# Attention with a folded projection: the scaling by 1/sum written back into PSUM, x added there, each as one VectorE operation

## The reference

```python
xn = (x - moving_mean) * jax.lax.rsqrt(moving_var + BN_EPS) * gamma + beta
q = xn @ Wq + bq
k = xn @ Wk + bk
v = xn @ Wv + bv
scores = jnp.einsum('bhid,bhjd->bhij', q, k) * d ** (-0.5)
attn = jax.nn.softmax(scores, axis=-1)
out = jnp.einsum('bhij,bhjd->bhid', attn, v)
out = out @ Wo + bo
return xn + out
```

## Time and profile before

| | us |
|---|---|
| median of 3 runs | 5316.65 |
| lowest, highest | 5316.29, 5316.69 |
| the profiled execution | 5315.75 |
| its span | 5313.9 |
| TensorE busy | 5260.1 |
| VectorE busy | 5029.7 |
| ScalarE busy | 4772.2 |
| GpSimd busy | 3642.2 |

### The profile page before, as it was taken

One profiled execution on the slowest core, in us unless ns is written; L12 is line 12 of the kernel. 1 busy time (PEld: TensorE's weight loads), 2 busy tenths in 40 slices (PEclk: granted clock), 3 DMA queues, 4 the chain that ended last, 5 costly groups with the idle time before them and its releaser, 6 DMA issues. The chain is left out here.

```text
span 5313.9 us, 177339 instructions
## 1 busy us (share of the span) xinstructions
PE 5260.1 (99%) x51224; PEld 4017.8 (76%) x51224; DVE 5029.7 (95%) x15394; ACT 4772.2 (90%) x19460; POOL 3642.2 (69%) x2056
## 2 busy tenths in 40 slices
PE   7999999999999999999999999999999999999999
PEld 5777777777777777777777777777777777777777
DVE  7999999999999999999999999999999999999998
ACT  6999999999999999999999999999999999999998
POOL 5666666666666666666666666666666666666665
PEclk9999999999999999999999999999999999999999
DMA  6777777777777777777777777777777777777776
GB/s 132 153 153 152 153 153 153 153 153 153 153 153 152 153 153 153 153 153 154 153 153 153 153 153 153 153 153 153 153 153 153 153 153 153 153 153 153 153 152 129
DMA packets 4294236, 806.27 MB, mean 152 GB/s; under 512 B 4294208, under 2 KB 4294208, under 8 KB 4294208
## 3 DMA queue, kind: packets, MB, share of 16 engines
q1 hardware_dynamic: 4294208, 805.93, 78.1%
HBM read 537.10 MB, written 268.44 MB: 152 GB/s over the span
## 5 line engine op out<-in xcount | busy, mean ns | idle before, releaser
L252 POOL TENSOR_TENSOR x_weighted<-x_in,row_weights 128x1024 f32<-128x1024 f32 x1024 | 2425.5, 2369 | 1554.9 <-issue 1159.7
L300 ACT ACTIVATE probs<-score_ps,neg_top 128x128 f32<-128x128 f32 x8192 | 2876.6, 386 | 0.0
L385 DVE SCALAR_TENSOR_TENSOR y<-o_ps,inv_sum,x_scaled_rows 128x64 f32<-128x64 f32 x8192 | 1665.5, 276 | 218.2 <-DVE inv_sum L378 213.3
L300 ACT ACTIVATION_READ_ACCUMULATOR probs<-score_ps,neg_top 128x1 f32 x8192 | 1854.2, 226 | 0.0
L461 PE MATMUL probsT_ps<-ident,probs 128*128 128x128 f32 x8192 | 1286.8, 280 | 2.5 <-ACT probs L300 2.0
L257 POOL TENSOR_TENSOR x_scaled_rows<-x_weighted,out_bias 128x512 f32<-128x512 f32 x1024 | 1216.0, 1187 | 90.7 <-POOL x_weighted L252 20.2
L392 DVE TENSOR_REDUCE row_stat<-score_ps 128x8 f32<-128x1024 f32 x1024 | 1244.2, 1215 | 6.5 <-PE score_ps L474 6.5
L474 PE MATMUL score_ps<-xT,g 64*128 64x128 f32 x16384 | 1190.8, 285 | 1.9 <-ACT g L284 1.9
L485 PE MATMUL u_ps<-probsT,x_in 128*64 128x128 f32 x16384 | 1120.6, 279 | 0.0
L474 PEld LDWEIGHTS score_ps<-xT,g 64*128 64x128 f32 x16384 | 994.6, 187 | 128.0 <-ACT g L284 5.0
L501 PE MATMUL g_ps<-xT,w_g 128*128 128x512 f32 x2048 | 1051.0, 595 | 2.9 <-DVE xT L425 2.9
(11 more groups left out here) (65 smaller groups left out, 1332.1 us busy)
## 6 DMA issues: line engine op xcount, KB each, us to landing
x_quads<-in_x SPq DMA_DIRECT2D x4096, 64.0 KB, 2.2
x_in<-in_x SPq DMA_DIRECT2D x1024, 256.0 KB, 2.9
out<-y SPq DMA_DIRECT2D x1024, 256.0 KB, 2.7
norm_row<-in_L_conv_gamma SPq DMA_DIRECT2D x1, 32.0 KB, 3.7
norm_row<-in_L_conv_beta SPq DMA_DIRECT2D x1, 32.0 KB, 3.7
norm_row<-in_L_conv_moving_mean SPq DMA_DIRECT2D x1, 32.0 KB, 4.2
norm_row<-in_L_conv_moving_var SPq DMA_DIRECT2D x1, 32.0 KB, 4.3
norm_row<-in_L_conv_bo SPq DMA_DIRECT2D x1, 32.0 KB, 4.3
```

Source lines behind the costliest of these rows:

```text
L252: nc.gpsimd.tensor_tensor(x_weighted[:, n % 2, :, 0:2 * C].rearrange("p s (h c) -> p s h c", h=2), x_in[:, n % 8, :, None, :].broadcast_to ...
L300: last = nc.scalar.activation(probs[:, n % 2, q, :], score_ps[n % 2][:, q // PAIRS, q % PAIRS * W:(q % PAIRS + 1) * W], ACT.Exp, bias=neg_ ...
L385: last = nc.vector.scalar_tensor_tensor(y[:, s, q, :], o_rows[:, q, :], inv_sum[:, s, q:q + 1], x_scaled_rows[:, n % 8, q, :], ALU.mult, A ...
```

## The change

It does four things.

- VectorE scales o in place: one operation of 128 x 512 reads o_ps and `inv_sum` (each value of it spread over 64 channels) and writes o_ps. It stands where L385's eight operations stood, and signals a new semaphore ring, `o_scaled`.
- One operation of 128 x 512 adds `x_scaled_rows` to o_ps and writes y. It stands behind the copy L401, and `y_found` is signalled there.
- The reciprocal stands at the end of the step before (n = t - 2) instead of at the start.
- ScalarE's first exponential of group t stands in front of L290, the copy of the second half of P of group t - 1; the other seven stay behind it.

TensorE's, GpSimd's and SP's instructions are the same.

```diff
@@ -109,6 +109,7 @@
         probsT_a_kept = sem_ring("probsT_a_kept")
         probsT_b_kept = sem_ring("probsT_b_kept")
         sum_inverted = sem_ring("sum_inverted")
+        o_scaled = sem_ring("o_scaled")
         x_weighed = sem_ring("x_weighed")
         x_scaled = sem_ring("x_scaled")
         y_found = sem_ring("y_found")
@@ -267,6 +268,24 @@
 
             probsT_rows = probsT_ps[:].rearrange("p (s w) -> p s w", s=HALF)
 
+            def exponentials(r, n, peeled, rows):
+                if not exists(r, n, peeled):
+                    return
+                s = parts(n)
+                if 0 in rows:
+                    act.wait_ge(neg_top_found[s], uses(r, n))
+                    if exists(r, n - 2, peeled):
+                        act.wait_ge(probsT_b_made[parts(n - 2)], uses(r, n - 2))
+                    if exists(r, n - 4, peeled):
+                        act.wait_ge(sum_inverted[s], uses(r, n - 4))
+                for q in rows:
+                    last = nc.scalar.activation(probs[:, n % 2, q, :], score_ps[n % 2][:, q // PAIRS, q % PAIRS * W:(q % PAIRS + 1) * W],
+                                                ACT.Exp, bias=neg_top[:, s, q:q + 1], accum_out=prob_sum[:, s, q:q + 1])
+                    if q == HALF - 1:
+                        last.then_inc(probs_a_found[s], 1)
+                    if q == GROUP - 1:
+                        last.then_inc(probs_b_found[s], 1)
+
             def step(r, t, peeled):
                 n = t - 1
                 if exists(r, n, peeled):
@@ -283,25 +302,13 @@
                         act.wait_ge(scores_made[s], uses(r, n - 4))
                     nc.scalar.activation(g[:, s].rearrange("p k w -> p (k w)"), g_ps[:],
                                          ACT.Identity, bias=g_bias[:, 0:1]).then_inc(g_kept[s], 1)
+                exponentials(r, t, peeled, range(0, 1))
                 n = t - 1
                 if exists(r, n, peeled):
                     s = parts(n)
                     act.wait_ge(probsT_b_made[s], uses(r, n))
                     nc.scalar.activation(probsT[:, n % 2, HALF:GROUP, :], probsT_rows, ACT.Copy).then_inc(probsT_b_kept[s], 1)
-                n = t
-                if exists(r, n, peeled):
-                    s = parts(n)
-                    act.wait_ge(neg_top_found[s], uses(r, n))
-                    if exists(r, n - 2, peeled):
-                        act.wait_ge(probsT_b_made[parts(n - 2)], uses(r, n - 2))
-                    if exists(r, n - 4, peeled):
-                        act.wait_ge(sum_inverted[s], uses(r, n - 4))
-                    for q in range(GROUP):
-                        last = nc.scalar.activation(probs[:, n % 2, q, :], score_ps[n % 2][:, q // PAIRS, q % PAIRS * W:(q % PAIRS + 1) * W],
-                                                    ACT.Exp, bias=neg_top[:, s, q:q + 1], accum_out=prob_sum[:, s, q:q + 1])
-                        if q == HALF - 1:
-                            last.then_inc(probs_a_found[s], 1)
-                    last.then_inc(probs_b_found[s], 1)
+                exponentials(r, t, peeled, range(1, GROUP))
 
             act.wait_ge(dve_setup, DVE_READY)
             pipeline(act, step)
@@ -374,17 +381,10 @@
                 n = t - 3
                 if exists(r, n, peeled):
                     s = parts(n)
-                    dve.wait_ge(probs_b_found[s], uses(r, n))
-                    nc.vector.reciprocal(inv_sum[:, s, :], prob_sum[:, s, :]).then_inc(sum_inverted[s], 1)
                     dve.wait_ge(sum_inverted[s], uses(r, n))
                     dve.wait_ge(o_made[s], uses(r, n))
-                    dve.wait_ge(x_scaled[s], uses(r, n))
-                    if exists(r, n - 4, peeled):
-                        dve.wait_ge(y_stored[s], dma_uses(r, n - 4))
-                    for q in range(GROUP):
-                        last = nc.vector.scalar_tensor_tensor(y[:, s, q, :], o_rows[:, q, :], inv_sum[:, s, q:q + 1],
-                                                              x_scaled_rows[:, n % 8, q, :], ALU.mult, ALU.add)
-                    last.then_inc(y_found[s], 1)
+                    nc.vector.tensor_tensor(o_rows, o_rows, inv_sum[:, s, :, None].broadcast_to([128, GROUP, C]),
+                                            ALU.mult).then_inc(o_scaled[s], 1)
                 n = t
                 if exists(r, n, peeled):
                     s = parts(n)
@@ -400,6 +400,14 @@
                         dve.wait_ge(o_made[parts(n - 2)], uses(r, n - 2))
                     nc.vector.tensor_copy(uT[:, n % 2], u_ps[:].rearrange("p (k w) -> p k w", k=PAIRS)) \
                         .then_inc(u_kept[s], 1)
+                n = t - 3
+                if exists(r, n, peeled):
+                    s = parts(n)
+                    dve.wait_ge(o_scaled[s], uses(r, n))
+                    dve.wait_ge(x_scaled[s], uses(r, n))
+                    if exists(r, n - 4, peeled):
+                        dve.wait_ge(y_stored[s], dma_uses(r, n - 4))
+                    nc.vector.tensor_tensor(y[:, s], o_rows, x_scaled_rows[:, n % 8], ALU.add).then_inc(y_found[s], 1)
                 n = t
                 if exists(r, n, peeled):
                     s = parts(n)
@@ -424,6 +432,11 @@
                         dve.wait_ge(scores_made[s], uses(r, n - 4))
                     nc.vector.transpose(xT[:, s].rearrange("p k w -> p (k w)"),
                                         x_quads[:, s].rearrange("p k w -> p (k w)")).then_inc(xT_kept[s], 1)
+                n = t - 2
+                if exists(r, n, peeled):
+                    s = parts(n)
+                    dve.wait_ge(probs_b_found[s], uses(r, n))
+                    nc.vector.reciprocal(inv_sum[:, s, :], prob_sum[:, s, :]).then_inc(sum_inverted[s], 1)
 
             pipeline(dve, step, dma=True)
 
```

## The result

The changed kernel takes 5444.28 us (median of 4 runs, 5443.72 to 5444.40) where the kernel before, on the same chip, takes 5316.47 (5315.96 to 5316.69): 1.024 times as long, with a 95% interval of 1.0223 to 1.0258. The forecast was 5438 us, in a range of 5365 to 5460. The profiled run took 5443.72.

What follows compares the result with a forecast made beforehand. The prediction took a loop between VectorE and TensorE to bound the kernel at 5.146 us a step; the new scores' loop sums to 5.265, and (5.265 - 5.146) x 1020 = 121 us more gives 5438 us, range 5365 to 5460.

Steps and rivals of the forecast that it cites:

- The loop: Scores to maximum, copy, addition, L509 and the next scores: a loop that closes without slack, 5.265 us a step; 75%.
- The terms: Pieces of one step around the scores' loop: 1.21, 1.14, 0.60, 0.68, 0.115 and 1.52, total 5.265 us.
- The release: From the addition's end to L509's weight load, waiting for y_found: 0.115 us, lower bound 0.06.
- The rival with the quick release: L509 released by y_found in 0.06 us like u_kept: step 5.21 us, time 5382 us; chance 12%.
- The addition's start: On VectorE, 0.60 us behind the copy L401's start; by the skill's page 0.08 later, 82 us more.
- Scaling in PSUM: VectorE's scaling of o_ps priced at 0.68 us; rival with slow PSUM writes, 1.13, 5530 us, chance 4%.
- Exponential and reciprocal at zero: Moving ScalarE's first exponential ahead of L290 and the reciprocal to the step's end costs nothing.
- Relief wins: Rival: VectorE's list falls by 0.34 us, TensorE sets the pace at 4.99 us a step, 5158 us; chance 5%.
- What the profile would show: L392 waits nearly every step, L509's wait blamed on the addition, uniform steps about 5.27 us, VectorE below 90%.

Runs made afterwards that it cites:

- e1: Changed kernel with the addition moved directly behind the scaling, ahead of the maximum L392: 5111.27 us, 0.9617 times the kernel before.
- e7: Changed kernel with a needless 128 x 256 product on VectorE between the copy of u and the addition: 5784.89 us, 1.0884 times the kernel before.
- e8: Changed kernel with a needless maximum over 128 x 256 elements directly behind the scaling: 5443.31 us, 1.0241 times the kernel before.
- e2: Changed kernel with the addition placed ahead of the copy of u, behind the maximum: 5379.07 us, 1.0121 times the kernel before.
- e3: Changed kernel with TensorE's two waits ahead of the old L509 written in exchanged order: 5379.62 us, 1.0122 times the kernel before.
- e4: Changed kernel with ScalarE's first exponential back behind the second copy of P: 5444.54 us.
- e5: Kernel before, eight operations kept, with only the first exponential in front and the reciprocal at the step's end: 5315.85 us, 0.9999 times the kernel before.
- e9: e1 with all eight exponentials behind the second copy of P again: 5111.37 us.

## Why the prediction was right, point by point

**The loop.** Named: the addition between the copy of u and L509's wait closes a loop over the scores. e1, which only moves the addition out of it, gains 333 us; e7, which puts work into it, pays it 1 to 1; e8, which puts work beside it, pays nothing.

**The terms.** L474 to L392 1.21 forecast and 1.21 measured; to the copy 1.14 and 1.14; to the addition 0.60 and 0.60; the addition 0.68 and 0.68; release 0.115 and 0.12; L509 to the next L474 1.52 and 1.52. The sum was 5.265; the mean of 1023 steps is 5.271. 0.006 x 1020 = 6 us is what the forecast was short, about what rows of two decimals leave open.

**The release.** It was read from two places of the setup where another wait of the same form ended. e2 and e3 show it to be a term of its own: 65 us of the 128. The rival with the quick release, 5382 us, is what e3 gives when the order of the two waits is exchanged, 5379.62. Without that term the forecast would have been the rival's 5382, 62 us short.

**The addition's start.** The prediction gives a sentence of the Trainium skill, page "VectorE: DVE Perf Modes", section "The DRAIN you can't avoid", by which the addition would start 0.08 later. It leaves out how that paragraph ends: a next operation that isn't held starts earlier. The trace agrees with the end: L410 starts 0.60 behind L401, which lasts 0.68, so the 82 us were rightly left out of the sum.

**Scaling in PSUM.** The price 0.68 was a little low, 0.70 measured, and writing PSUM costs no double time. The room behind it held (e8).

**Exponential and reciprocal at zero.** e4, e5 and e9 bear it out within 1 us; the reciprocal's place was tried in e5 alone, on the kernel before. The idle time ahead of the second copy vanished as said, but not ScalarE's waiting: it moved to the first copy (L296, 342.1 us over the run).

**Relief wins, the rival with 5158 us.** It did not come in the changed kernel. Its figure for what would then set the step, 4.99 us, was wrong. It adds the place of L509's first product, 3.47, to the 1.52 that is counted from L509's weight load. In the earlier trace rows product and load start together, in e1 the load is 0.09 ahead, at 3.38, and 3.38 + 1.52 = 4.90. e1's short steps have 4.91, its mean is 4.948. The 3.47 itself held: in e1 the product doesn't start earlier either. Where TensorE's own floor lies was not measured; e1 is still bound by the loop over o_ps. The forecast doesn't use this figure.

**What the profile would show.** The steps are uniform at 5.27 and L392 waits in each, as said; VectorE's share is 88%. One sign was named wrongly: that L509's wait would be put down to the addition. The view puts it down to the copy, for the reason that e3 shows.

## What to carry to other kernels

Follow the loop between engines that closes once a step, and add up the edges; an engine with idle time can still be slowed by where a new operation stands in its queue, and sped up by 6% by nothing but another place for one operation. Signal the buffer that another engine waits for before starting work that nobody waits for. Where an instruction waits for two semaphores, let the one that comes last ride on the instruction, here by writing its wait first: that alone was 65 us in 5444. When you add up a path from rows, count every piece between the same kind of points, from weight load to weight load or from product to product: here the two lay up to 0.09 us apart.

## What the runs showed of the hardware that was not expected

- A product of two SBUF operands, 128 x 256, took 1.24 us on VectorE when it started 1.4 us into GpSimd's L254, and 0.42 when only the last 0.06 us of GpSimd's L259 lay beside it. The scaling and the addition, with one operand in PSUM each, took 700 and 681 ns in the mean of a run in which GpSimd was busy 67% of the time.
- A weight load whose separately waited semaphore comes last starts 0.12 behind the end of the signalling instruction (changed kernel), one that carries the semaphore itself 0.05 to 0.06 (e1, e2, e3).
- VectorE's operation from PSUM into the same place of PSUM took 0.02 us more than one from PSUM to SBUF (700 against 681 ns for 512 elements, L386 and L410).
- In e1 the addition, which waits for the scaling's write, starts 0.73 behind the scaling in six steps of ten and 0.82 to 0.84 in the others. What decides between them stays open.
